# Every second tile of the routed experts loaded by rows and transposed on TensorE

## What is computed

```python
N_EXPERTS, TOP_K, MOE_INTER, HIDDEN = 32, 6, 128, 256
topk_idx, topk_w = router(x, gate_w, e_bias)          # 6 of 32 experts for each of 4096 tokens
combine = zeros((T, N_EXPERTS)).at[arange(T)[:, None], topk_idx].add(topk_w)
h = square(relu(einsum('th,eih->tei', x, up_w)))      # up: 256 -> 128 features for each expert
h = h * combine[:, :, None]
moe_out = einsum('tei,ehi->th', h, down_w)            # down: 128 -> 256
```

## Time and profile before

| | us |
|---|---|
| median of 3 runs | 1739.87 (1739.26 to 1742.06) |
| the profiled execution's own time | 1734.04 |
| its span, first to last instruction | 1732.2 |
| of that the tile loop, first transposing load issued to last store issued | 570.1 to 870.8 |

### The profile page before, as it was taken

One profiled execution on the slowest core, in us unless ns is written; L12 is line 12 of the kernel. 1 busy time (PEld: TensorE's weight loads), 2 busy tenths in 40 slices (PEclk: granted clock), 3 DMA queues, 4 the chain that ended last, 5 costly groups with the idle time before them and its releaser, 6 DMA issues. The chain is left out here.

```text
span 1732.2 us, 21636 instructions
## 1 busy us (share of the span) xinstructions
PE 1050.4 (61%) x7253; PEld 663.4 (38%) x7253; DVE 982.8 (57%) x2161; ACT 592.3 (34%) x997; POOL 481.8 (28%) x472
## 2 busy tenths in 40 slices
PE   0374665466550566676613667787878787867666
PEld 0142443244330444555501234453544454534343
DVE  4466665675561344544434755767686777765543
ACT  3231213121320233333310243544545353535433
POOL 0116446644655000000064633333323241200000
PEclk9977877688785789989955687998989898989887
DMA  6803122322222799999935334343434343321000
GB/s 212 304 29 118 68 88 93 110 73 88 82 80 93 184 231 233 236 230 247 238 116 117 102 86 105 81 105 91 107 80 118 77 120 72 78 44 45 26 25 25
DMA packets 242874, 201.68 MB, mean 116 GB/s; under 512 B 153424, under 2 KB 211536, under 8 KB 242768
## 3 DMA queue, kind: packets, MB, share of 16 engines
q1 hardware_dynamic: 219728, 133.18, 32.3%
q0 software_dynamic: 20736, 58.75, 10.4%
q10 hardware_dynamic: 2304, 8.39, 1.3%
HBM read 69.44 MB, written 84.15 MB: 89 GB/s over the span
## 5 line engine op out<-in xcount | busy, mean ns | idle before, releaser
L1628 DVE TENSOR_REDUCE row_max<-bank 128x2 f32<-128x512 f32 x256 | 174.9, 688 | 176.9 <-PE bank L1370 174.2
L1732 POOL DMA_INDIRECT y_in<-ys,y_row x192 | 198.7, 1035 | 195.7 <-DVE x_tok L1588 139.3
L884 POOL DMA_INDIRECT xs<-x_row,slot_row x192 | 193.4, 1007 | 103.8 <-issue 53.8
L1510 ACT ACTIVATE prob<-bank 128x512 f32<-128x512 f32 x256 | 152.1, 594 | 138.0 <-PE bank L1389 138.0
L1389 PE MATMUL bank<-q_stack,k_stack 98*128 98x256 f16 x512 | 108.5, 296 | 113.1 <-ACT prob L1510 80.0
L309 PE MATMUL bank<-xt_tile,w_hi 128*128 128x256 f16 x512 | 98.7, 295 | 102.9 <-DMA xt_tile<-xs 102.8
L309 PE MATMUL bank<-ct,w_hi 128*128 128x512 f16 x128 | 56.1, 533 | 134.8 <-DVE ct L698 126.8
L1115 DVE TENSOR_TENSOR hid_tile<-relu_tile 128x512 f32<-128x512 f32 x64 | 44.3, 693 | 163.3 <-ACT relu_tile L1033 163.1
L1726 POOL TENSOR_TENSOR rstd<-var_eps,minus_half 128x4 f32<-128x4 f32 x16 | 16.5, 1033 | 380.2 <-DVE var_eps L664 380.2
L1370 PE MATMUL bank<-k_stack,q_stack 96*128 96x256 f16 x512 | 109.8, 300 | 19.7 <-DVE k_stack L1719 10.5
L1033 ACT ACTIVATE relu_tile<-bank 128x512 f32<-128x512 f32 x64 | 38.2, 597 | 240.5 <-PE bank L309 240.5
(11 more groups left out here) (198 smaller groups left out, 2771.8 us busy)
## 6 DMA issues: line engine op xcount, KB each, us to landing
ys<-y_tile SPq DMA_DIRECT2D x128, 256.0 KB, 3.0
stage<-in_weights SPq DMA_DIRECT2D x21, 477.0 KB, 4.2
xs<-zeros SPq DMA_DIRECT2D x32, 256.0 KB, 5.3
inverse<-den_mid SPq DMA_DIRECT2D x64, 128.0 KB
ctx_t<-in_ctx SPq DMA_DIRECT2D x8, 512.0 KB, 5.1
x_tok<-in_x SPq DMA_DIRECT2D x8, 512.0 KB, 4.4
ct_mid<-ct SPq DMA_DIRECT2D x8, 512.0 KB, 3.1
x_mid<-x_tok SPq DMA_DIRECT2D x8, 512.0 KB, 2.8
```

The lines of the kernel that those rows point to most:

```text
L884: nc.gpsimd.indirect_dma_start(xs[:, :], bass.IndirectOffsetOnAxis(slot_row[p][:, tt, k:k + 1], axis=0), x_row[p][:, tt, :, :].rearrange(" ...
L1510: nc.scalar.activation(prob[:, h % NPR, :, :], seconds.bank(f"{bb}exp{h}")[:, :], ACT.Exp, scale=float(HD) ** -0.5) \
L1628: V.tensor_reduce(row_max[:, :, h], firsts.bank(f"{b}max{h}")[:, :].rearrange("p (q k) -> p q k", q=2), AX_X, ALU.max).then_inc(firsts.rea ...
L1732: nc.gpsimd.indirect_dma_start(y_in[:, k % 3, tt, :], None, ys[:, :], bass.IndirectOffsetOnAxis(y_row[:, g * TT + tt, k:k + 1], axis=0)) \
```

## The change

Even tiles are loaded as before, by the transposing DMA. Odd tiles are loaded by a plain DMA into a new buffer `row_tile`, two successive rows of `xs` (2 KB) to a partition. TensorE transposes them in half precision into `tab_bank` with eight 128x128 transposes (`turn_rows`), and ScalarE copies the 128x1024 result into the odd half of `xt_tile` (`turned_rows`). The tile's rows now stand in another order (even rows, then odd rows), and the store of an odd tile undoes it: each partition writes two successive rows, 2 KB in one piece, where it wrote two pieces of 1 KB.

```diff
@@ -915,6 +915,7 @@
             y_top = sb("y_top", [P, GROUPS * TT, 8], to=second)
             NX, NH, NY = 3, 3, 4
             xt = [sb(f"xt_tile{b}", [P, 2, 2 * DT, TILE], F16, second) for b in range(NX)]
+            rows = [sb(f"row_tile{b}", [P, 2, 2 * D], F16, second) for b in range(NX)]
             relu = sb("relu_tile", [P, 2, 2 * TILE], to=second)
             hid = sb("hid_tile", [P, 2, 2 * TILE], to=second)
             hid_hi, hid_lo = (sb(f"hid_tile_{n}", [P, NH, 2 * TILE], F16, second) for n in ("hi", "lo"))
@@ -929,6 +930,8 @@
             counts_in = sem("t_counts_in")
             tabled, tab_full, tab_in = sem("t_tabled"), sem("t_tab_full"), sem("t_tab_in")
             x_loaded = [sem(f"t_x_loaded{b}") for b in range(NX)]
+            rows_loaded = [sem(f"t_rows_loaded{b}") for b in range(NX)]
+            rows_full, rows_turned = sem("t_rows_full"), sem("t_rows_turned")
             up_full, relu_done, hid_done = (sem(f"t_{n}") for n in ("up_full", "relu_done", "hid_done"))
             hid_hi_done, hid_lo_done = sem("t_hid_hi_done"), sem("t_hid_lo_done")
             down_full, y_done = sem("t_down_full"), [sem(f"t_y_done{j}") for j in range(2)]
@@ -956,17 +959,21 @@
 
                 def store(tile):
                     sp.wait_ge(y_done[tile % 2], tile // 2 + 1)
-                    sp.dma_start(ys[tile * TILE:(tile + 1) * TILE, :].rearrange("(h p) d -> p h d", p=P),
+                    order = "(h p) d -> p h d" if tile % 2 == 0 else "(p h) d -> p h d"
+                    sp.dma_start(ys[tile * TILE:(tile + 1) * TILE, :].rearrange(order, p=P),
                                  y[:, tile % NY, :, :]).then_inc(stored[tile % NY], 16)
 
                 for n in range(PAIRS + 4):
                     if n < PAIRS:
                         if 2 * n % BATCH_TILES == 0:
                             row_of += entries(sp, 0, 2 * n // BATCH_TILES, sets, EXPERTS * ROOM - TILE)
+                        wait(sp, rows_full, n - NX + 1)
+                        sp.dma_start(rows[n % NX][:, :, :],
+                                     xs[bass.ds(row_of[2 * n + 1], TILE), :].rearrange("(p h) d -> p h d", h=2)) \
+                          .then_inc(rows_loaded[n % NX], 16)
                         wait(sp, up_full, n - NX + 1)
-                        for j in range(2):
-                            sp.dma_start_transpose(xt[n % NX][:, j, :, :], xs[bass.ds(row_of[2 * n + j], TILE), :]) \
-                              .then_inc(x_loaded[n % NX], 16)
+                        sp.dma_start_transpose(xt[n % NX][:, 0, :, :], xs[bass.ds(row_of[2 * n], TILE), :]) \
+                          .then_inc(x_loaded[n % NX], 16)
                     if n >= 4:
                         for j in range(2):
                             store(2 * (n - 4) + j)
@@ -990,8 +997,20 @@
                 pe.wait_ge(tab_in, 1)
                 col_of = []
 
+                def turn_rows(n):
+
+                    pe.wait_ge(rows_loaded[n % NX], 16 * (n // NX + 1))
+                    wait(pe, rows_turned, n)
+                    bank = tab_bank[:, :].bitcast(F16)
+                    for c in range(2 * DT):
+                        for h in range(2):
+                            mm = pe.transpose(bank[:, c * TILE + h * P:c * TILE + (h + 1) * P],
+                                              rows[n % NX][:, h, c * P:(c + 1) * P], ident16[:, :])
+                    mm.then_inc(rows_full, 1)
+
                 def up(n):
-                    pe.wait_ge(x_loaded[n % NX], 32 * (n // NX + 1))
+                    pe.wait_ge(x_loaded[n % NX], 16 * (n // NX + 1))
+                    pe.wait_ge(rows_turned, n + 1)
                     wait(pe, relu_done, n - 2)
                     for j in range(2):
                         at = WEIGHTS["up"][1]
@@ -1019,6 +1038,10 @@
                     if n < PAIRS:
                         if 2 * n % BATCH_TILES == 0:
                             col_of += entries(pe, 1, 2 * n // BATCH_TILES, sets, (EXPERTS - 1) * D)
+                        if n == 0:
+                            turn_rows(0)
+                        if n + 1 < PAIRS:
+                            turn_rows(n + 1)
                         up(n)
                     if n >= LAG:
                         down(n - LAG)
@@ -1026,7 +1049,17 @@
             @block.scalar
             def _(act):
                 n1 = STAGE[1]
+
+                def turned_rows(n):
+                    act.wait_ge(rows_full, n + 1)
+                    wait(act, up_full, n - NX + 1)
+                    nc.scalar.activation(xt[n % NX][:, 1, :, :].rearrange("p c t -> p (c t)"), tab_bank[:, :].bitcast(F16),
+                                         ACT.Copy).then_inc(rows_turned, 1)
+
+                turned_rows(0)
                 for n in range(PAIRS + LAG):
+                    if n + 1 < PAIRS:
+                        turned_rows(n + 1)
                     if n < PAIRS:
                         act.wait_ge(up_full, n + 1)
                         wait(act, hid_done, n - 1)
```

## The result

The changed kernel takes 1757.03 us in the median of 5 runs (1751.02 to 1760.97), the kernel before 1739.87 us (1737.18 to 1742.06, 5 runs). The ratio is 1.0094, with a 95% interval from 1.0068 to 1.0119. The forecast was 1731 us, in a range from 1705 to 1753.

The account below looks back on a forecast made before the run. The prediction took the DMA engines, at 93%, with the register reload, to bound the kernel before, and the ring afterwards. Six blocks -12, weight turns +8, ordinary turns -4, drain -1 gave -9 us: 1731 us, range 1705 to 1753.

Parts of the forecast that it names:

- the ring of two turns: Tile loop: row load, transposes, products, store of an old pair, next row load wait in a circle; 8.2 us per two pairs.
- the last block and the drain: End of the tile loop: the last of six blocks that together gain 12 us, and a drain one ring shorter, -1 us.
- Four rounds are 32.8 us: Block of eight turns: four passes through the ring at 8.2 us each, before the reload's share.
- 34.0 us for a block: Eight turns of the tile loop: 32.8 us plus 1.2 for the reload, where it was 36.0; six blocks give -12 us.
- 0.7 + 4.0: Within the ring: transposes 0.7 us, then 4.0 us from the start of the up products to the odd `y_tile`.
- L = 2.9: Row load, issue to landing: 2.9 us, with ends 2.0 and 3.7; later landing decides from 3.2 us on.
- The clock rival: TensorE in the loop: if transposes did not count as work, mostly half clock, +100 us, 1840 us; chance 0.04.
- The reload: SyncE's register reload each eighth turn: 2.5 us, counted half, 1.2 us, since one of two interleaved rings takes the delay.
- The weight turns: First 16 turns, SyncE waiting for the split of a weight piece: 2.8 us more for each of the last three, +8.
- The ordinary turns in between: Nine turns among the first 16: from about 4.3 to about 3.9 us, as SyncE catches up after a stall, -4 us.
- the row load lands late: Rival: the ring with landing at 3.7 us, some 27 rounds each 0.8 longer, +22 on -9, 1753 us; chance 0.25.
- L = 3.7: Upper end for the row load's issue to landing, as the weight piece and, at 3.8, the transposing load show under load.

Follow-up runs that it names:

- e1: Changed kernel with the row load of pair n+1 issued one turn earlier on SyncE; 0.9771 of the kernel before, tile loop 268.0 us.
- changed, again: The changed kernel, unchanged, run and profiled a second time beside the follow-up runs; 1.0074 of the kernel before, tile loop 321.7 us.
- e9: Kernel before with only the odd tiles' stores changed to two successive rows (2 KB) to a partition; 1.0017 of the kernel before.
- e3: Changed kernel with the row load moved behind the transposing load of the same pair on SyncE; 1.0495 of the kernel before, loop 401.0 us.
- e6: Changed kernel with row loads one turn ahead and weight pieces two turns later; 0.9683 of the kernel before, tile loop 252.3 us.

## Why the prediction was wrong

The mechanism was named: the ring of two turns, its order and its parts, and e1 shows that it costs the time. Its length was wrong, and so was what disturbs it. The forecast of -9 us came from three stretches; the first profiles show how each went:

| stretch of the loop | forecast, us | measured, us |
|---|---|---|
| first 16 turns | +4 | +15.7 |
| the next five blocks of eight | -10 | +5.1 |
| the last block and the drain | -3 | +6.3 |
| sum | -9 | +27.1 |

**The blocks.** *"Four rounds are 32.8 us" and "34.0 us for a block"*: this step failed. The five blocks take 39.0, 36.5, 37.6, 36.3 and 35.6 us, in the mean 37.0, where the kernel before took 36.0. Each round can be divided at the landing of its row load, its first transpose and the end of its odd `y_tile`. These are the means of the 38 rounds that begin in the 17th to the 54th turn:

| part of a round | forecast, us | changed | changed, again |
|---|---|---|---|
| row load, issue to landing | 2.9 | 3.37 | 3.35 |
| from there to the first transpose | nothing | 0.22 | 0.18 |
| first transpose to odd `y_tile` | 0.7 + 4.0 | 4.73 | 4.63 |
| to the next row load, with the reload's share | 0.6 + 0.3 | 0.91 | 0.93 |
| sum | 8.5 | 9.23 | 9.09 |

- *L = 2.9* is the term that cost most: 0.47 of the 0.73 us a round, 1.9 us for a block. The prediction had named 3.2 as the point from which it would fail.
- *From landing to the first transpose* the sum had nothing. Two rings share TensorE. Where turns are unequal, the load of the second lands while TensorE is still in the turn of the first, for up to 1.65 us.
- *0.7 + 4.0* came out by luck. At full clock this part is 4.5 us, less than forecast; the turns at half clock bring the mean to 4.7. The clock rival had assumed that most of the loop would be at half clock, and the forecast none of it; it came in single turns. In both profiles of the changed kernel together, the three blocks without such a turn take 35.6, 34.4 and 36.5 us, still more than 34.0, the other seven 36.3 to 39.0. So half clock is a part of the miss and not the whole.
- *The reload*, counted half, held: the last row of the table is right.

**The first 16 turns.**

- *The weight turns*: the four take 45.6 us where they took 31.4, +14.2 where +8 was forecast. Two held to the tenth: the turn of pair 7, from 600.98 to 611.75, 10.8 us, and that of pair 11, 9.3. The first, left out of the forecast, took 12.9 where it had taken 8.1. The one from 649.56 took 12.6: its load landed after 3.4 us, and the transposes then waited another 1.3 us for TensorE, which was working at half clock on the turn ahead of it.
- *"The ordinary turns in between ... to about 3.9, since SyncE catches up after a stall"*: failed. In the weight turns TensorE had waited 7.2 to 7.9 us and then ran at half clock, and the round 611.75 to 621.49 took 9.7 us. The nine ordinary turns average 4.8 where they had averaged 4.3: +3.8 where -4 was forecast. The first three turns, not in the forecast, are 2.3 us shorter.

**The last block and the drain.** They take 48.6 us where they took 42.3. The last row load's landing stands ahead of `up(62)`, so TensorE has one turn more to do behind the last load than before. That load took 6.0 us to land, the longest of all 64, and its transposes begin at 884.11 behind a wait of 3.2. In the second profile it landed after 4.8, and block and drain are 45.8 us. This is read from the traces only.

**What held, and what is open.** The eight transposes take 0.6 us, the copy 1.02, the plain load's issue 0.34. A turn of SyncE with its stores is never under 3.0 us, where 2.75 was forecast; that binds nothing here. What bounds the kernel before stays open: the prediction took the DMA engines for it, the change lightens both them and SyncE's queue, and no run separates the two. With the ring gone, the lighter load is worth 34 us of the loop (e1).

The rival "the row load lands late" had the sign and nearly the time, 1753, but by luck: it rests on L = 3.7. With the measured 3.4 its own rule, 27 rounds, gives 13 or 14 us on -9, so about 1744. The rest of the 1757 came from the weight turns, the drain, the half clock and the shared TensorE, which it did not have.

The loop's growth in the first profiles is 27.1 us and in the second ones 19.5; the medians differ by 17.2, since the first profile of the changed kernel is of the slowest of its runs. How much each part would give back by itself isn't settled, since they overlap.

## What to carry to other kernels

A transfer that is made cheaper helps only if it is also issued early enough. Where a new step puts a load of pair n+1 ahead of the work on pair n, the load must be issued a turn earlier too: with it the change is worth 2.3%, without it it costs 0.7 to 0.9%. With the weight pieces moved too it is 3.2%, of which the kernel before gains 0.5% without the change. A ring should be summed with the mean landing under its own load and for its disturbed rounds as well (reloads, side loads, the clock behind a wait); here the two interleaved rings stayed unequal for several turns after each disturbance. And a run that is to price a cheaper step should first be looked at for whether the step became cheaper: in e9 it hadn't.

## What the hardware showed that I had not expected

In e3, where TensorE waited ahead of every second turn, mostly 2.5 to 5.1 us, the mean granted clock of a stretch was 0.78, and 18 useless products of 256 columns in each such wait brought it to 0.94 and the loop from 401.0 to 371.9 us (one profile each). Eight half-precision transposes took 0.61 us at full clock and 1.03 us at half; they did not keep the clock down in a loop full of products: in e6, with 8 transposes among 24 products per turn, it was 0.98. A store of 256 KB in 2 KB pieces right behind another store was issued in 0.47 us in the median (e9), just as in 1 KB pieces.
